# A Strassen layer whose weight sums and residual are made by accumulating transfers in DRAM

## The reference

```
def _sage_layer(h, edge_src, edge_dst, deg_inv, W_self, W_neigh, b):
    msg = h[edge_src]
    agg = segment_sum(msg, edge_dst, num_segments=h.shape[0])
    mean = agg * deg_inv[:, None]
    return h @ W_self + mean @ W_neigh + b
...
    h = relu(_sage_layer(x, src, dst, deg_inv, W_self0, W_neigh0, b0))
    out = _sage_layer(h, src, dst, deg_inv, W_self1, W_neigh1, b1)
...
x = x + gnn(layernorm(x), src, dst, ...)
x = x + ffn(layernorm(x)[None], ...)[0]
```

## Time and profile before

| | us |
|---|---|
| median of 3 runs | 1112.87 (1103.74 to 1113.25) |
| the profiled execution | 1110.37 |
| its span | 1108.6 |
| TensorE busy | 1048.8 (95%) |
| VectorE busy | 732.3 (66%) |
| ScalarE busy | 467.3 (42%) |
| GpSimd busy | 331.6 (30%) |

### The profile page before, as it was taken

One profiled execution on the slowest core, in us unless ns is written; L12 is line 12 of the kernel. 1 busy time (PEld: TensorE's weight loads), 2 busy tenths in 40 slices (PEclk: granted clock), 3 DMA queues, 4 the chain that ended last, 5 costly groups with the idle time before them and its releaser, 6 DMA issues.

```text
span 1108.6 us, 17295 instructions
## 1 busy us (share of the span) xinstructions
PE 1048.8 (95%) x5765; PEld 929.2 (84%) x5765; DVE 732.3 (66%) x1192; ACT 467.3 (42%) x1042; POOL 331.6 (30%) x285
## 2 busy tenths in 40 slices
PE   5999999999999998989998999999999989999995
PEld 4999999999999996767686777889999679999994
DVE  6678888888752338988538789553221468878883
ACT  5555434453311222435203334454332257777772
POOL 5500000000000226656506683002442124554532
PEclk9999999999999999999998999999999889999998
DMA  7332133213227772333135422465565087999971
GB/s 190 95 106 71 44 107 108 73 46 99 71 71 217 204 208 64 112 138 114 49 111 150 143 85 68 138 198 160 154 182 190 20 310 237 318 307 288 307 219 30
DMA packets 76803, 160.80 MB, mean 145 GB/s; under 512 B 13315, under 2 KB 38141, under 8 KB 72221
## 3 DMA queue, kind: packets, MB, share of 16 engines
q1 hardware_dynamic: 65053, 128.42, 36.2%
q0 software_dynamic: 10976, 30.74, 10.7%
q10 hardware_dynamic: 672, 0.32, 0.1%
HBM read 124.32 MB, written 42.96 MB: 151 GB/s over the span
## 4 chain that ended last, share of the span: by engine, by line
PE 74%; DVE 9%; issue 7%; POOL 3%; DMA 3%; ACT 2%; DVEq 1%; SPq 0%; POOLq 0%; ACTq 0%
PE ps L1065 14%; PE ps L1717 10%; PE ps L2364 9%; PE ps L1679 8%; PE ps L1377 7%; PE ps L2385 6%; PE ps L1664 5%; PE ps L910 4%; PE ps L824 3%; PE ps L2350 2%; POOL bw_lo L1299 2%; POOL bw_sum L1285 1%; ACT hs_hi L1361 1%; DVE hs_sum L1334 1%; DVE hs_sum L1342 1%
## 5 line engine op out<-in xcount | busy, mean ns | idle before, releaser
L1285 POOL TENSOR_TENSOR bw_sum<-bw_sum,bw_raw 128x512 f32<-128x512 f32 x40 | 60.9, 1533 | 337.4 <-DMA bw_raw<-in_L_gnn_W_self 294.9
L1664 PE MATMUL ps<-bw_hi,hs_hi 128*125 128x512 f32 x280 | 114.9, 410 | 19.4 <-POOL bw_lo L1299 10.8
L917 DVE TENSOR_TENSOR adj<-ps,adj 125x250 f32 x212 | 88.1, 416 | 41.6 <-PE ps L910 33.5
L1664 PE MATMUL ps<-bw_hi,hs_lo 128*125 128x512 f32 x280 | 112.4, 402 | 0.0
L1664 PE MATMUL ps<-bw_lo,hs_hi 128*125 128x512 f32 x280 | 112.4, 401 | 0.0
L1065 PE MATMUL ps<-h_lo,w_hi 128*128 128x418 f32 x336 | 108.5, 371 | 0.0
L1299 POOL TENSOR_TENSOR bw_lo<-bw_sum,bw_hi 128x512 fp32r<-128x512 f32 x56 | 83.4, 1495 | 81.0 <-ACT bw_hi L1293 81.0
L1065 PE MATMUL ps<-h_hi,w_hi 128*128 128x418 f32 x336 | 100.3, 379 | 0.0
L2458 DVE TENSOR_TENSOR w_lo<-w_raw,w_hi 128x2048 fp32r<-128x2048 f32 x34 | 77.8, 2289 | 25.6 <-ACT w_hi L2413 22.1
L1065 PE MATMUL ps<-h_hi,w_lo 128*128 128x418 f32 x336 | 93.4, 359 | 0.0
L1377 PE MATMUL ps<-adj,y_hi 125*128 125x416 f32 (+1 forms) x240 | 85.9, 358 | 1.7 <-DMA self<-self_d 1.2
(11 more groups left out here) (306 smaller groups left out, 2679.8 us busy)
## 6 DMA issues: line engine op xcount, KB each, us to landing
w_raw<-in_L_ffn_ew SPq DMA_DIRECT2D x34, 1024.0 KB, 7.9
bw_sum<-in_L_gnn_W_neigh SPq DMA_DIRECT2D x20, 512.0 KB, 5.7
bw_raw<-in_L_gnn_W_self SPq DMA_DIRECT2D x16, 512.0 KB, 4.8
xin<-in_x SPq DMA_DIRECT2D x10, 448.0 KB
t_d<-xn SPq DMA_DIRECT2D x10, 448.0 KB
base<-x_d POOLq DMA_DIRECT2D x10, 448.0 KB, 4.4
out<-base POOLq DMA_DIRECT2D x10, 448.0 KB, 3.4
y_d<-y_hi SPq DMA_DIRECT2D x7, 625.0 KB
```

The costliest lines, as they stand in the source:

```text
L917: e.tensor_tensor(cols, ps[0:P, 5 + b % 2, 0:KW].rearrange("p (t w) -> p t w", t=NT), cols, ALU.add).then_inc(self.took, 1)
L1285: e.tensor_tensor(own, own, bw_raw[:, k, :], ALU.subtract if FORM(g) in (3, 4) else ALU.add).then_inc(bw_s, 1)
L1664: mm = e.matmul(ps[0:P, bank, :], ht[slot_of(n)][:, k, :], wt[u][:, k, :], start=(form not in ONTO and k == 0 and i == 0), stop=(k == KH - ...
```

## The change

Five of the seven forms have a summed weight block; after the change only form 1 is still summed in SBUF. At the start of the first layer, once `adj` is cleared, GpSimd issues 8 transfers that copy a 512 x 512 block (1 MB) from the weights to a scratch tensor `sum_d` in DRAM, and one that writes b1 to all 1250 rows of `xb_d` (5.1 MB). When all nine have landed it issues nine transfers that add the second block to each sum, and x to `xb_d`. SP waits for all 18 before the first block load. Signs of the node sums are turned so that the sums in DRAM are all additions and form 1 is a subtraction. The residual rows are loaded from `xb_d`, and the additions of the bias on GpSimd are gone, with the loads of b1 and the semaphore `s_x`. The low parts of all 14 weight blocks move from GpSimd to VectorE: block 0 at i = 3 and block 1 at i = 5 of the aggregation, block 8 (the second of the second half) at j = 8 between the halves, all others inside the halves, three in the iterations p = 2, 3, 4 of the group before and the fourth in iteration p = 0 of the group itself. GpSimd keeps the four sums of form 1 in each half. The hunks below stand in the order: constants, GpSimd's transfers behind the memsets, the source of the block loads, the residual load, SP and VectorE in the aggregation, GpSimd's loop, VectorE's `taken` and the end of its iteration.

```diff
-SUMMED_B = (1, 3, 4, 6, 7)
+SUMMED_B = (1,)
+ADDED = (3, 4, 6, 7)
+NADD = NQ * len(ADDED)
...
+        def weight_block(q, form, i):
+            v, low_half = BLOCKS_OF[form][i]
+            return N1_W[v][D // 2 * low_half:D // 2 * (low_half + 1), HALF * q:HALF * (q + 1)]
...
+            added = [(q, i, form) for q in range(NQ) for i, form in enumerate(ADDED)]
+            for q, i, form in added:
+                e.dma_start(sum_d[len(ADDED) * q + i], weight_block(q, form, 0)).then_inc(s_sums, 16)
+            e.dma_start(xb_d, I["L0_gnn_b1"].partition_broadcast(N)).then_inc(s_sums, 16)
+            e.wait_ge(s_sums, 16 * (NADD + 1))
+            for q, i, form in added:
+                e.dma_start(sum_d[len(ADDED) * q + i], weight_block(q, form, 1), accum_op=ALU.add).then_inc(s_sums, 16)
+            e.dma_start(xb_d, I["x"], accum_op=ALU.add, max_dma_last_dim=4 * D).then_inc(s_sums, 16)
...
+            if i == 0 and form in ADDED:
+                rows = sum_d[len(ADDED) * q + ADDED.index(form)]
+            else:
+                rows = weight_block(q, form, i)
+            return view(rows)[:, 2 * k:2 * k + 2, :]
...
-            by_rows(e, s_rows1[:, t:t + n, :], x_view[:, t:t + n, HALF * q:HALF * q + HALF], s_in[g])
+            by_rows(e, s_rows1[:, t:t + n, :], xb_view[:, t:t + n, HALF * q:HALF * q + HALF], s_in[g])
...
                 if i == 1:
                     e.wait_ge(x_full, 3 * KT)
                     e.wait_ge(z_full, 3 * KT + 3)
+                    e.wait_ge(s_sums, 32 * (NADD + 1))
                     block_load(e, 0)
-                    raw_load(e, 0)
-                if i == 3:
-                    bias_load(e, 0)
-                if i == 4:
-                    raw_load(e, 1)
                 if i == 5:
                     block_load(e, 1)
...
+                if i in (3, 5):
+                    for k in range(KH):
+                        block_low(e, i // 5, k)
...
             def prepare(g):
-                block_sum(e, g, 0)
-                block_sum(e, g, 1)
-                block_low(e, g, 0)
-                block_sum(e, g, 2)
-                block_low(e, g, 1)
-                block_sum(e, g, 3)
-                block_low(e, g, 2)
-                block_low(e, g, 3)
...
+                for k in range(KH):
+                    block_sum(e, g, k)
+
+            for g in range(NQ * MS):
                 prepare(g)
...
-                    e.wait_ge(s_x, 3 * q + 1 + p // 4)
+                    e.wait_ge(s_in[p // 4], 32 * q + 32)
...
+                    g, p = divmod(n0 + i, PAIRS)
+                    if i >= 2 * PAIRS and p == 0 and g < NQ * MS:
+                        block_low(e, g, KH - 1)
+                    if PAIRS <= i < UNITS and p > 1 and g + 1 < NQ * MS:
+                        block_low(e, g + 1, p - 2)
```

More of the change, by code:

```diff
@@ L439, in build @@
         t_d = nc.dram_tensor("t_d", (N, D), F32, kind="Internal").ap()
+        xb_d = nc.dram_tensor("xb_d", (N, D), F32, kind="Internal").ap()
+        sum_d = nc.dram_tensor("sum_d", (NADD, D // 2, HALF), F32, kind="Internal").ap()
+        s_sums = sem("s_sums")
         s_id = sem("s_id")
@@ L1246, in build @@
         s_st = [sem(f"s_st{g}") for g in range(3)]
-        N1_W = (I["L0_gnn_W_neigh1"], I["L0_gnn_W_self1"])
         nat = lambda a: a.rearrange("(t p) n -> p t n", p=P)
-        x_view, x2_view = nat(I["x"]), nat(x2_d)
+        xb_view, x2_view = nat(xb_d), nat(x2_d)
         tile_of = lambda i: slice(i * P, (i + 1) * P)
         group_of = lambda i: min(i // 4, 2)
-        BLOCKS_OF = {1: ((0, 0), (1, 1)), 2: ((0, 0), None), 3: ((1, 0), (1, 1)), 4: ((0, 1), (0, 0)),
-                     5: ((1, 1), None), 6: ((0, 0), (1, 0)), 7: ((0, 1), (1, 1))}
         def half_block(g, i, k):
-            v, low_half = BLOCKS_OF[FORM(g)][i]
-            a = HALF * (g // MS)
-            return view(N1_W[v])[:, KH * low_half + 2 * k:KH * low_half + 2 * k + 2, a:a + HALF]
+            q, form = g // MS, FORM(g)
+            if i == 0 and form in ADDED:
[3 more added lines that the diff above has]
+            return view(rows)[:, 2 * k:2 * k + 2, :]
         def block_load(e, g):
@@ L1284, in block_sum @@
                 e.wait_ge(raw_in[k // 2], 16 * sums_b_to(g) + 16)
-                e.tensor_tensor(own, own, bw_raw[:, k, :], ALU.subtract if FORM(g) in (3, 4) else ALU.add).then_inc(bw_s, 1)
+                e.tensor_tensor(own, own, bw_raw[:, k, :], ALU.subtract).then_inc(bw_s, 1)
         def block_high(e, g, k):
@@ L1922, in taken @@
                 if form == 3:
-                    e.wait_ge(s_x, 3 * q + 1 + p // 4)
+                    e.wait_ge(s_in[p // 4], 32 * q + 32)
                     onto(own)
                 if form == 6:
-                    e.wait_ge(s_x, 3 * q + 2 + (p + PAIRS) // 8)
+                    e.wait_ge(s_in[1 + (p + PAIRS) // 8], 32 * q + 32)
                     onto(other)
@@ L2001, in _ @@
                             nodes_low(e, n0 + UNITS + 1)
+                            for k in range(KH):
+                                block_low(e, MS + 1, k)
                         continue
```

37 lines of the change are left out of this document (7 added, 30 removed).

## The result

The changed kernel took 1146.3 us in the median (1142.31 to 1151.72), the kernel before 1111.2 beside it on the same chip: a ratio of 1.033, 95% interval [1.027, 1.040]. Executions in the chip's slower state (two in experiment 4, one each in 6 and 8, of 10, 4 and 10) are left out of the ratios, not of the medians. The forecast was 1130 us in a range of 1088 to 1158, slower with a chance of 0.53. The profiled execution took 1142.3 us against 1110.4, so 31.9 us more, and the two parts that the prediction weighed against each other are both in it, both larger than forecast.

The account below looks back on a forecast made before the run. The prediction took TensorE, 74% of the chain of waits, to bound the kernel. From the profiled 1110.4 us it took 21 for the halves and added 41 for the sums' traffic: 1130 us, range 1088 to 1158.

Parts of the forecast that it names:

- 41: First layer: us lost to the DRAM sums' traffic delaying neighbour slabs and stopping TensorE, clock included; bounds 12 and 73.
- The halves, -21: Strassen layer's two halves: 29 us of TensorE waits and clock to be had, less 8 that stay; bounds 13 and 29.
- three tight places: VectorE in the halves: late block low parts 3 us, second half's form 7 group 2.5, z_lo wait 2.
- D: Rival: DRAM sums come too late, SP stands at s_sums, TensorE stops some 40 us; 1170 us, chance 0.05.
- d: First layer: delay of a neighbour slab by the software queue's packets; 8, 15, 15 and 8 us over four bursts.
- The "highest" bound: Slab delay if all 122 packets on its path each let a foreign one by: 26 us in accumulation.
- The 2.6 us that I let be absorbed: First layer: the part of a ScalarE wait for the slab that does not stop TensorE, 2.6 us.
- the clock 4.8: First layer: TensorE's slower clock after its stops, counted as three times 1.6 us.
- A: Rival: the sums get by without delaying the slabs, so the kernel is faster; 1089 us, chance 0.24.
- B: Rival: a draw, slab delays of 6 to 10 us everywhere, losses of 12 to 28; 1101 to 1118 us, chance 0.20.
- the zero slack: First layer: the neighbour slab lands exactly when ScalarE wants it; 2.09 us already waited once, 0.5 us slack another time.
- C: Rival: VectorE becomes the pace of the halves, eating the 21 us; 1151 with the delays, 1110 without; chance 0.07.

Follow-up runs that it names:

- experiment 4: The kernel before, with SP issuing the next neighbour slab's load ahead of the stores of y and self: 1107.2 us, ratio 0.999.
- experiment 6: The changed kernel in its own queue order, with only the y stores cut so that they run on 16 engines: 1125.3 us, ratio 1.012.
- 8: The kernel before, with only the weight blocks' low parts moved to VectorE; GpSimd keeps its 40 sums and the bias: 1097.3 us, ratio 0.992.
- experiment 7: The changed kernel with rows of at most 1,024 bytes asked for in all 18 transfers: 1133.8 us, ratio 1.022.
- 3: The changed kernel, with SP issuing the next neighbour slab's load ahead of the stores of y and self: 1115.1 us, ratio 1.006.
- experiment 5: The changed kernel with the neighbour slab's load ahead of the stores and each y store cut to run on 16 and 13 engines: 1085.3 us, ratio 0.981.

## Why the prediction came out as it did

The mechanism and the sign were right: the traffic delays the slab, ScalarE's wait stops TensorE, and that outweighs the halves. Both sizes were too small, and their errors cancel in part: 1110.4 - 21 + 41 = 1130 was forecast, 1110.4 - 31 + 63 = 1142 came. That the total is 12 us off while its terms are 10 and 22 off is luck.

**The halves, -21: measured 31.** The terms listed for what was to be had (21.5 of waits, then 1.6, 4.6, 1.1 and 1.6 of clock) add up to 30.4 and not to 29; it doesn't matter for the result. Windows of the halves of 101 to 105 us were forecast and 103.3 and 102.6 came; VectorE at 87 to 90 us came at 84 to 85, with 26 and 22 instructions more where 24 and 20 were forecast. The 8 us that were to stay in three tight places were too many: bw_lo has 3.8 us in three waits instead of 5.5 in ten, z_lo 0.5 instead of 2. Within the two windows the gain was 23.0 us, close to the 21; most of the other 8 lies outside them. The aggregation between them takes 43.7 us for 47.6 and the stretch ahead of the first takes 111.1 for 114.7: part of the z_lo wait and of its clock was counted, but not the whole of the clock of 0.96 in the aggregation and of 0.99 ahead of the layer, or a 1.2 us wait for self_d.

**When the traffic runs.** Copies were forecast to end by about 110 us, and GpSimd's wait for them ended at 114.8 (the 55.3 us above); all was over at some 212 us, forecast about 200 to 215. SP never waited for it, so D is out: accumulation between two places in DRAM ran at 2048 B in 0.178 us on an engine, 11.5 bytes/ns where 9.6 was taken. Three bursts met it, not four, because the stops themselves moved the later bursts apart (67, 132 and 189 us instead of every 34).

**The step that failed: d.** I took 8, 15, 15 and 8 us. It was 29.5, 21.3 and 13.6 (45.0, 36.8 and 29.1 less 15.5). The term was mis-sized by its count: I let between a half and all of the packets on the slab's path meet a foreign one. The "highest" bound was the right count: every packet on the path, the rows of 512 bytes too, lets one by. With 122 packets and the 0.178 us of an accumulating packet that is 21.7, and 21.3 came. For the copies the upper bound was 13 us, 122 times the 0.107 of a 2 KB packet; yet their packets were larger, 4096 B in 0.159 us in the median, and some took much longer: from 70 to 112.8 us the foreign packets took 0.240 us in the mean, a tenth of them over 0.49. 122 times 0.240 is 29.3, and 29.5 came. The long ones lie mostly after 86 us, when the broadcast of the bias was under way; that it made them long is not shown. The third burst was shorter because the traffic ran out under it. This is seen from the other side too: in the first burst 159 packets of 5120 B (0.196) begin in 12.5 us on the five store engines, so they follow each other by 0.39 us, which leaves room for one foreign packet between them; without the traffic they follow each other by 0.2 us (50 in 2 us). The counts in 6 and 7 (709 to 705, 548 to 542) say the same of the small rows. The profile doesn't say on which engine a packet ran, so these are counts over all 16. A rival, that the memory as a whole held things up and not the turns, would make SP's own packets longer; they grew from 0.196 to 0.211 and from 0.027 to 0.041 us, less than 2 us over the slab's path.
The Trainium skill (DMA: Bandwidth & Descriptors, Queues, rings and completion order) has an engine drain a packet of typically 9 to 17 descriptors from one ring before it turns. By it, read as in the prediction with one foreign packet a turn, the slab's small rows would have got by in a few turns and d would have been 13.5. The traces don't agree: 21.3, the count one for one; and experiment 7, where the second wait followed the length of a foreign packet. I cannot say from these runs whether the sentence fails for small rows of any queue or of SP's alone.

**What a wait costs TensorE.** The 2.6 us that I let be absorbed are exact: ScalarE's 32.2, 21.7 and 14.0 became TensorE's 29.6, 19.1 and 11.4. For the clock 4.8 was taken, and 4.4 us are left beside the waits.

**The rivals.** A (the sums get by) and B (a draw) fell with the zero slack: the slack was as small as read, since ScalarE's waits (32.2 with the 2.1 it had before, 21.7, 14.0) are the delays of 29.5, 21.3 and 13.6 to within 0.6 us. C (VectorE becomes the pace) fell: 85 of 103 us. With the traffic gone the kernel runs at 1082, close to A's 1089: its value was near, its condition wasn't met.

**Where the loss could be taken back.** Not in the traffic (experiment 7) but in the queue that it delays, and in two steps: the order moves the delay from the slab to the stores (3), the width takes it from the stores (5), and neither alone is enough (3: 1115; 6: 1125; both: 1085). The best kernel of this study is that of experiment 5, 1.9% under the kernel before and 17 us under the same queue without the change. Not tried: the sums in a place with idle DMA engines, and what is left of the 9.7 us.

## What to carry to other kernels

In this kernel work that was moved to the DMA engines was not paid where it was issued but by what landed just in time on those engines meanwhile. So before a bulk transfer is added, look in the trace for the load with the least slack, count the packets on its path on the busiest engine, its own queue's stores included, and multiply by the mean length of one foreign packet. When such a load is late, first look at what stands ahead of it in its own queue and on how many engines that runs; then look at whoever waits for what was pushed back. And take the gain of a relieved engine from the whole stretch between two marks, not from the waits alone: the clock behind each wait came back too.

## What the runs showed of the hardware

- Packets of SP's queue and of GpSimd's went by one for one, rows of 512 bytes (0.027 to 0.041 us each) included: 705 beside 709 in 15 us of experiment 6, and 122 packets beside foreign ones of 0.178 us each were 21.3 us late.
- Copies from DRAM to DRAM with rows of 2 KB went in packets of 4096 B at 0.159 us, and stayed so when rows of at most 1,024 bytes were asked for. Accumulating transfers kept the rows: 1024 B in 0.102 us, 2048 B in 0.178, 4000 B in 0.320. Byte for byte accumulation thus took about twice the time of a copy (2048 B in 0.178 against 4096 B in 0.159), and shorter rows cost more in all (two of 1024 B 0.204, one of 2048 B 0.178).
- The bias row broadcast to 5 MB took 55.9 us from issue to landing behind the eight copies, as the last transfer of its phase, and GpSimd's wait of 55.3 us was for it. The issues, KB each and median us to landing:

```profile
sum_d<-in_L_gnn_W_self POOLq DMA_DIRECT2D x8, 1024.0 KB, 24.9
sum_d<-in_L_gnn_W_neigh POOLq DMA_DIRECT2D x8, 1024.0 KB, 19.4
...
xb_d<-in_L_gnn_b POOLq DMA_DIRECT2D x1, 5000.0 KB, 55.9
xb_d<-in_x POOLq DMA_DIRECT2D x1, 5000.0 KB, 36.5
```

- GpSimd did not issue all accumulating transfers at once: the last one started after 53.2 us idle, for nothing that the profile names ("issue"), at 176.4 us, 0.8 us after the last packet of the eight sums had begun. In this kernel GpSimd had nothing else to do there.
